# Recommender tower: block transposes and four of a chunk's 50 summations on VectorE, part of the last layer 1 earlier

## The reference, cut to what matters

```python
# 2048 samples, 40 fields; each field has a table of 1000 to 125000 rows of 32 floats
e = jnp.stack([tbl_0[ids[:, 0]], ..., tbl_39[ids[:, 39]]], axis=1)        # 2048 x 40 x 32
z = einsum('bke,kef,bkf->bk', e[:, I], W, e[:, J])                       # 780 pairs i < j, W is 780 x 32 x 32
h = concatenate([z, dense_ctx], axis=1)                                  # 796 columns
h = maximum(h @ W_top1 + b_top1, 0)                                      # 512
h = maximum(h @ W_top2 + b_top2, 0)                                      # 256
y = h @ W_top3                                                           # 1
```

## Time and profile before

| | us |
|---|---|
| median of 3 runs | 684.99 (684.2 to 687.2) |
| profiled execution, its own time | 685.17 |
| its span | 683.6 |
| TensorE busy (share of the span) | 660.2 (97%) |
| VectorE busy | 522.0 (76%) |
| ScalarE busy | 232.9 (34%) |
| GpSimd busy | 433.1 (63%) |

### The profile page before, as it was taken

How to read it: one execution, slowest core, us unless ns; L and a number is a source line. 1 busy time by engine, 2 the same in 40 slices (tenths; PEclk the granted TensorE clock), 3 DMA queues, 4 the chain that set the end, 5 groups by cost and what they waited for, 6 DMA issues and landing times.

```text
span 683.6 us, 13973 instructions
## 1 busy us (share of the span) xinstructions
PE 660.2 (97%) x5920; PEld 192.6 (28%) x5920; DVE 522.0 (76%) x483; ACT 232.9 (34%) x200; POOL 433.1 (63%) x452
## 2 busy tenths in 40 slices
PE   5679999999999999999999999999999999999998
PEld 1222323222322333222332233322222222222232
DVE  5687889999967668778987887568978778688900
ACT  6636675164554338630164313501010110010002
POOL 6777777777777777777777777777777774000000
PEclk9999999999999999999999999999999999999999
DMA  7832022111221021111222102001022210000000
GB/s 261 299 87 60 14 75 75 18 26 29 78 62 30 14 60 33 41 29 30 45 52 57 45 14 45 13 15 30 14 57 50 46 29 9 16 17 0 3 3 1
DMA packets 26454, 32.22 MB, mean 47 GB/s; under 512 B 10436, under 2 KB 18372, under 8 KB 26136
## 3 DMA queue, kind: packets, MB, share of 16 engines
q1 hardware_dynamic: 11736, 23.41, 11.1%
q0 software_dynamic: 14336, 7.37, 7.1%
q10 hardware_dynamic: 320, 0.56, 0.3%
HBM read 20.75 MB, written 0.06 MB: 30 GB/s over the span
## 4 chain that ended last, share of the span: by engine, by line
PE 94%; ACT 3%; DVE 1%; issue 1%; DMA 1%; ACTq 0%; DVEq 0%
PE t_ps L637 30%; PE z_ps L667 27%; PE x_ps L686 11%; PE x_ps L597 9%; PE t_ps L686 4%; PE t_ps L645 3%; PE x_ps L699 3%; PE x_ps L613 2%; PE t_ps L597 2%; ACT one_hot L460 1%; ACT one_hot L463 1%; PE x_ps L710 1%; PE t_ps L699 1%; DMA z_sb<-hot_tables 1%; DVE prod L555 0%
## 5 line engine op out<-in xcount | busy, mean ns | idle before, releaser
L555 DVE TENSOR_TENSOR prod<-t_ps,e_t 128x1024 f32<-128x1024 f32 x400 | 466.8, 1218 | 107.8 <-PE t_ps L637 76.1
L415 POOL DMA_INDIRECT rows<-tbl,idx x448 | 432.9, 966 | 139.9 <-issue 135.9
L637 PE MATMUL t_ps<-e_t,w_sb 32*128 32x512 f32 x1440 | 219.8, 640 | 1.1 <-DVE prod L555 1.0
L667 PE MATMUL z_ps<-prod,select 128*32 128x512 f32 x1600 | 207.8, 600 | 2.3 <-DVE prod L555 1.8
L637 PEld LDWEIGHTS t_ps<-e_t,w_sb 32*128 32x128 f32 x1440 | 65.9, 182 | 140.1 <-DVE prod L555 75.0
L460 ACT ACTIVATE one_hot<-hot_sb,row_number 128x2048 bf16<-128x2048 f16 (+1 forms) x44 | 85.4, 1940 | 36.6 <-PE x_ps L597 34.7
L686 PE MATMUL x_ps<-z_sb,w_sb 128*32 128x512 f32 x672 | 83.4, 597 | 0.7 <-ACT e_t L472 0.7
L463 ACT ACTIVATE one_hot<-one_hot 128x2048 bf16<-128x2048 bf16 (+1 forms) x44 | 81.5, 1853 | 1.4
L597 PE MATMUL x_ps<-one_hot,tables 128*32 128x512 bf16 x1074 | 72.7, 387 | 1.7 <-DVE tables L521 1.0
L667 PEld LDWEIGHTS z_ps<-prod,select 128*32 128x32 f32 x1600 | 39.3, 108 | 122.1 <-issue 61.6
L497 ACT COPY z_sb<-z_ps 128x512 f32<-128x512 f32 x28 | 16.4, 586 | 159.3 <-PE z_ps L667 159.2
(11 more groups left out here) (27 smaller groups left out, 83.8 us busy)
## 6 DMA issues: line engine op xcount, KB each, us to landing
rows<-tbl,idx POOLq DMA_INDIRECT x448, 2.3
hot_sb<-hot_ids SPq DMA_DIRECT2D x10, 512.0 KB
e_t<-e_t SPq DMA_DIRECT2D x80, 64.0 KB
e_t<-e_t SPq DMA_DIRECT2D x40, 128.0 KB
w_sb<-w_lay SPq DMA_DIRECT2D x1, 1792.0 KB
z_sb<-hot_tables SPq DMA_DIRECT2D x4, 320.0 KB, 6.2
w_sb<-w_lay SPq DMA_DIRECT2D x1, 1152.0 KB, 8.8
w_sb<-w_lay SPq DMA_DIRECT2D x1, 896.0 KB, 6.2
```

The lines of the kernel that those rows point to most:

```text
L415: pool.indirect_dma_start(out=rows[:, slot, t, E * f:E * f + E], out_offset=None, in_=tables[PER * c + f], in_offset=bass.IndirectOffsetOn ...
L555: nc.vector.tensor_tensor(prod[:, u % PROD_SLOTS, :, :], t_ps[:, at:at + 2, :], by, ALU.mult).then_inc(mult_done, 1)
L637: mm = nc.tensor.matmul(t_ps[:, at + r % 2, :], w_sb[part, b, :], e_t[part, e_slot(k, g), :], start=True, stop=True)
L667: mm = nc.tensor.matmul(z_ps[E * q:E * q + E, :], select[:, E - PER - PER * s:2 * E - PER - PER * s], prod[:, u % PROD_SLOTS, q % 2, :], s ...
```

## The change

- **Block transposes.** `turn` goes from TensorE to VectorE (L654): one instruction transposes 128 x 512 in blocks of 32 x 32 straight into `e_t`, and the copy by ScalarE goes. So that blocks are enough, a gather now fetches 32 samples of all four fields (4 x 32 rows, from one table in which the 28 large ones lie end to end), still 16 for an item, 448 in all. VectorE first adds each table's first row to the indices (L593), and GpSimd and the first cast (L596) come behind that addition.
- **Sums.** Bursts 9, 19, 25 and 31 of each chunk are not summed by `red`, but by VectorE (L663): a `tensor_reduce` that transposes blocks, one for each unit of 1024 elements, 32 in all. A block transpose (L671) brings a chunk's sums into z's layout, and an addition (L684) joins them with the four bursts of the same bank that `red` summed; it takes the place of ScalarE's copy of that bank.
- **Early layer 1.** In the last chunk banks 0 to 3 of layer 1 go through `x_ps` among the bursts, ScalarE keeps them in `h1_sb`, and VectorE adds them to the rest (L677).
- **Halves.** All `gen` steps are 8 products of 32 x 64, as those of L645 were.
- **Layer 3** is 4 products over 128 samples in four column groups (L829).
- **The string ORDER is new.** 70 of the 112 one-hot matrices are made by ScalarE (44 before), 42 by VectorE (68 before). In the list, between the first burst of chunk 0 and that of chunk 1 stand now 48 lookup blocks (43 before), 45 summations (48), 8 `turn` (7), 11 one-hot matrices on VectorE (25) and 8 sums; behind the first burst of chunk 1 stand 20 `turn` (21), 139 summations (152), 110 `layer1` (112) and 48 lookup blocks (50).

```diff
+HOT = [3, 3, 3, 3]
...
+CHUNKS = 4
+EARLY = 4
+SMALL = Z_BANKS - 2
+SMALL_SLOTS = BATCHES - (Z_BANKS - 1) * Z_SLOTS
+SUMMED = [9, 19, 25, 31]
+REDUCED = [b for b in range(len(BURSTS)) if b not in SUMMED]
+JOINED = SMALL - 1
+DENSE_AT = PER * SMALL_SLOTS
...
+def z_place(b):
+    if b in SUMMED:
+        return JOINED, Z_SLOTS - len(SUMMED) + SUMMED.index(b)
+    n = REDUCED.index(b)
+    if n >= SMALL * Z_SLOTS - len(SUMMED):
+        n += len(SUMMED)
+    if n >= SMALL * Z_SLOTS + SMALL_SLOTS:
+        n += Z_SLOTS - SMALL_SLOTS
+    return divmod(n, Z_SLOTS)
...
-    layer1 += [("layer1", chunks - 1, m, kb) for kb in range(Z_BANKS) for m in range(H1_TILES)]
+    layer1 += [("layer1", chunks - 1, m, kb) for m in range(H1_TILES) for kb in range(EARLY)]
+    layer1 += [("layer1", chunks - 1, m, kb) for kb in range(EARLY, Z_BANKS) for m in range(H1_TILES)]
...
+        "r": [("red", k, b) for k in range(chunks) for b in REDUCED],
+        "d": [("sum", k, b, half) for k in range(chunks) for b in SUMMED for half in range(2)],
+        "a": [("join", k) for k in range(chunks if SUMMED else 0)],
+        "t": [("turn", k, c) for k in range(chunks) for c in range(HOT[k], GROUPS)],
...
+        if k == CHUNKS - 1 and step[3] < EARLY:
+            return ("h1 early", k, step[2]), step[3] == 0, step[3] == EARLY - 1
+        return ("h1", k, step[2]), step[3] == (EARLY if k == CHUNKS - 1 else 0), step[3] == Z_BANKS - 1
...
+    GATHER = 16 * SPANS
...
+        idx = sb("idx", [P, len(items), SPANS], I32)
+        idx_raw = sb("idx_raw", [P, len(items), SPANS], I32)
+        if SUMMED:
+            sums = sb("sums", [P, SPANS, Z_SLOTS, PER])
...
+        def wait_for_products(engine, u):
+            if u >= PROD_SLOTS:
+                k, b = divmod((u - PROD_SLOTS) // 2, len(BURSTS))
+                if b in SUMMED:
+                    engine.wait_ge(sum_done, summed_to(k, b, u % 2))
+                else:
+                    engine.wait_ge(red_done, reduced_to(k, b))
...
-            pool.wait_ge(idx_loaded, 16)
-            for n, (k, c) in enumerate(items):
+            pool.wait_ge(idx_made, 1)
+            for n in range(len(items)):
                 slot = n % ROW_SLOTS
                 if n >= ROW_SLOTS:
-                    pool.wait_ge(x_made, use_no["e", *items[n - ROW_SLOTS]] + 1)
-                for t in range(TILES):
-                    for f in range(PER):
-                        pool.indirect_dma_start(
-                            out=rows[:, slot, t, E * f:E * f + E], out_offset=None,
-                            in_=tables[PER * c + f],
-                            in_offset=bass.IndirectOffsetOnAxis(
-                                ap=idx[:, k * TILES + t, PER * c + f:PER * c + f + 1], axis=0),
-                        ).then_inc(gathered[slot], 16)
+                    pool.wait_ge(turned, n - ROW_SLOTS + 1)
+                for span in range(SPANS):
+                    pool.indirect_dma_start(
+                        out=rows[:, slot, span, :], out_offset=None, in_=table,
+                        in_offset=bass.IndirectOffsetOnAxis(ap=idx[:, n, span:span + 1], axis=0),
+                    ).then_inc(gathered[slot], 16)
...
+                    if use[0] == "h1 early":
+                        nc.scalar.copy(h1_sb[:, m, :], bank_of(use)).then_inc(x_taken, 1)
+                    else:
+                        into = bank_of(use)
+                        if k == chunks - 1:
+                            act.wait_ge(h1_joined, m + 1)
+                            into = h1_sb[:, m, :]
+                        nc.scalar.activation(h1_sb[:, m, :], into, ACT.Relu,
+                                             bias=b1_sb[:, m:m + 1]).then_inc(x_taken, 1)
...
-                    nc.scalar.copy(y_sb[:, :], x_ps[0:1, :]).then_inc(x_taken, 1)
+                    nc.scalar.copy(y_sb[:, :], x_ps[:, 0:P]).then_inc(x_taken, 1)
...
+                nc.vector.memset(sums[:, :, :, :], 0.0).then_inc(sums_cleared, 1)
+            dve.wait_ge(idx_loaded, 16)
+            dve.wait_ge(numbers_loaded, 16)
+            nc.vector.tensor_tensor(idx[:, :, :], idx_raw[:, :, :], first_row.unsqueeze(2).broadcast_to(idx.shape),
+                                    ALU.add).then_inc(idx_made, 1)
...
+                elif kind == "turn":
+                    c = step[2]
+                    n = item_no[k, c]
+                    dve.wait_ge(gathered[n % ROW_SLOTS], (n // ROW_SLOTS + 1) * GATHER)
+                    wait_for_place(dve, k, c)
+                    nc.vector.transpose(e_t[:, e_slot(k, c), :],
+                                        rows[:, n % ROW_SLOTS, :, :].rearrange("p s e -> p (s e)")).then_inc(turned, 1)
+                elif kind == "sum":
+                    b, half = step[2:]
+                    u = first_unit(k, b) + half
+                    kb, s = z_place(b)
+                    dve.wait_ge(mult_done, u + 1)
+                    if b == SUMMED[0] and half == 0:
+                        dve.wait_ge(z_turned, k) if k else dve.wait_ge(sums_cleared, 1)
+                    nc.vector.tensor_reduce(sums[:, :, s, 2 * half:2 * half + 2].rearrange("p n q -> p q n"),
+                                            prod[:, u % PROD_SLOTS, :, :].rearrange("p q (n e) -> p q n e", e=E),
+                                            axis=mybir.AxisListType.X, op=ALU.add,
+                                            apply_transpose=True).then_inc(sum_done, 1)
+                    if b == SUMMED[-1] and half:
+                        bank = k * Z_BANKS + kb
+                        dve.wait_ge(sum_done, summed_to(k, b, half))
+                        wait_for_z_place(dve, bank)
+                        nc.vector.transpose(z_sb[:, bank % Z_RING, :],
+                                            sums[:, :, :, :].rearrange("p n s q -> p (n s q)")).then_inc(z_turned, 1)
+                elif kind == "layer1" and k == chunks - 1 and step[3] == Z_BANKS - 1:
+                    m = step[2]
+                    dve.wait_ge(x_taken, use_no["h1 early", k, m] + 1)
+                    dve.wait_ge(x_made, use_no["h1", k, m] + 1)
+                    nc.vector.tensor_tensor(h1_sb[:, m, :], t_ps[:, tail_banks["h1", k, m], :], h1_sb[:, m, :],
+                                            ALU.add).then_inc(h1_joined, 1)
+                elif kind == "join":
+                    bank = k * Z_BANKS + JOINED
+                    last = max(b for b in REDUCED if z_place(b)[0] == JOINED)
+                    dve.wait_ge(z_turned, k + 1)
+                    dve.wait_ge(red_done, reduced_to(k, last))
+                    nc.vector.tensor_tensor(z_sb[:, bank % Z_RING, :], z_ps[:, :], z_sb[:, bank % Z_RING, :],
+                                            ALU.add).then_inc(z_read, 1)
...
-            def turn(step):
-                _, k, c = step
-                use, _, _ = use_of(step)
-                open_bank(use)
-                slot, rounds = item_no[k, c] % ROW_SLOTS, item_no[k, c] // ROW_SLOTS
-                pe.wait_ge(gathered[slot], (rounds + 1) * GATHER)
-                for t in range(TILES):
-                    mm = nc.tensor.transpose(x_ps[:, t * P:(t + 1) * P], rows[:, slot, t, :], ident[:, :])
-                mm.then_inc(x_made, 1)
...
-                    pe.wait_ge(x_taken, use_no["e", k, g] + 1)
+                    wait_for_e(pe, k, g)
...
-                    if g < c:
-                        mm = nc.tensor.matmul(t_ps[:, at + r % 2, :], w_sb[part, b, :], e_t[part, e_slot(k, g), :],
+                    near = far = e_slot(k, g)
+                    if g == c:
+                        near, far = e_slot(k, c + r // 2), fold_slot(k, c + r // 2)
+                    for side in range(2):
+                        source = far if (r, side) in ((1, 0), (3, 1)) else near
+                        cols = slice(P // 2 * side, P // 2 * side + P // 2)
+                        mm = nc.tensor.matmul(t_ps[cols, at + r % 2, :], w_sb[part, b, cols], e_t[part, source, :],
                                               start=True, stop=True)
-                    else:
-                        near, far = e_slot(k, c + r // 2), fold_slot(k, c + r // 2)
-                        for side in range(2):
-                            source = far if (r, side) in ((1, 0), (3, 1)) else near
-                            cols = slice(P // 2 * side, P // 2 * side + P // 2)
-                            mm = nc.tensor.matmul(t_ps[cols, at + r % 2, :], w_sb[part, b, cols], e_t[part, source, :],
-                                                  start=True, stop=True)
...
-                mm = nc.tensor.matmul(x_ps[0:1, :], w3_sb[:, j:j + 1], h2_sb[:, j, :], start=first, stop=ends)
+                for q in range(PER):
+                    mm = nc.tensor.matmul(x_ps[E * q:E * q + 1, 0:P], w3_sb[:, j:j + 1], h2_sb[:, j, P * q:P * q + P],
+                                          start=first, stop=ends)
...
```

(22 more changed lines are left out.)

152 lines of the change are left out of this document (86 added, 66 removed).

## The result

| | us |
|---|---|
| predicted | 646.0 (637 to 660) |
| measured, median of 4 runs | 644.37 (643.69 to 646.65) |
| the kernel before on the same chip, median of 4 | 685.34 (684.2 to 687.2) |
| ratio, with its 95% interval | 0.9406 (0.9373 to 0.9438) |
| the profiled execution of the changed kernel, its span | 646.65, 644.9 |

A forecast was written before the change was run, and what follows sets the result against it. The prediction took TensorE's list of steps as the bound over the whole, VectorE as chunk 0's pace. It summed 35.8 + 0.9 (start) + 145 (chunk 0) + 460.8 (rest) + 2 (waits) = 644.5 and predicted 646 us, range 637 to 660.

The forecast's parts named there:

- TensorE's list: TensorE's steps over the whole kernel: they bound the time and lose 41.6 us, from 683.6 to 642.0.
- The turns: 28 transposes leaving TensorE at 0.58 us each: 16.2 us, and 1.4 us that they waited.
- The halves: 180 `gen` steps in halves, 1.05 us against 1.08: 3.6 us off TensorE, bounds 0 and 5.4.
- Layer 3: 8 TensorE steps with column groups side by side, 0.95 to 0.3 us each: 5.2 us, and 0.3 at the end.
- The summations: 16 summations (4 x 4) leaving TensorE at 0.93 us each: 14.9 us.
- Early layer 1 removes nothing: Last chunk: 16 steps, 14 us, move ahead of the last product, and TensorE's list keeps its length.
- VectorE's list: VectorE over the whole: loses 19.0 us of one-hot matrices, gains 65.4 us of new work, 568 us busy.
- Over the whole it does not bind: VectorE's floor, 568 + 14 + 21 = 603 us, lies 39 us under TensorE, so VectorE isn't the bound.
- Chunk 0 in 145 us: First to 201st product: VectorE sets the pace, 140 us of work and 3% idle, against 149.8 before.
- The start: Ahead of the first product: the cast comes behind the index addition, moving the start and every gather by 0.9 us.
- The rest: From chunk 1's first product to the end: 498.0 less 37.2 us is 460.8, and 2 for `gen` waits behind sums.
- The costlier coupling: Rival: sums of up to 2.3 us and other VectorE work hold up the products, 654 to 672 us; chance 0.15.

The follow-up runs named there:

- run 5: Changed kernel with 28 times four TensorE transposes, whose result nothing reads, added beside VectorE's block transposes: 660.39 us, 16.0 slower than the changed kernel.
- run 2: Changed kernel with the 180 `gen` steps between different groups in full width again, 4 products of 128 columns: 647.8 us, 3.4 slower.
- run 4: Changed kernel with layer 3 again as one product over 512 samples in one column group: 648.26 us, 3.9 slower.
- run 1: Changed kernel with no burst summed by VectorE, all 50 of each chunk summed by TensorE: 674.76 us, 30.4 slower.
- run 3: Changed kernel without early layer 1, its 16 steps back behind the last product: 651.23 us, 6.9 slower.
- run 6: Changed kernel with each of VectorE's 32 sums made twice, the second into a spare tile: 674.9 us, 30.5 slower.
- run 8: Changed kernel with the first cast ahead of the index addition and a second id spread step earlier: 642.83 us, 1.5 faster.
- run 7: Changed kernel with the 8 sums of chunk 0 cut to 32 of their 512 samples: 642.73 us, 1.6 faster.

## Why the prediction was right, and where it wasn't

- **TensorE's list.** Right: near 620 us forecast as busy, 618.5 measured. The turns were 16.2 us, and run 5 gives 16.0. The halves were 3.6, and run 2 gives 3.4. The Trainium skill, "TensorE: Matmul & The Clock Gate", Part 3, lets a weight load overlap matrix products in flight only where the row group differs, and the two halves share theirs. A `gen` in halves at 1.04 us, against 1.08 in full width, does not agree with it. Layer 3 was 5.5 with its smaller copy, and run 4 gives 3.9, though a step takes 0.22 and not my 0.3; part of a whole step runs beside its successor.
- **The summations.** 14.9 for 16 of them, 0.93 each. The undisturbed chunks of run 1 give 3.4 us for four, 0.85 each, which would be an estimated 13.6 for 16. The 30.4 of the whole run hold waits at the bank that the move itself made.
- **"Early layer 1 removes nothing; TensorE's own list keeps its length".** Wrong. It is worth 6.9 us (run 3). The two passages before it in my own text say why: a pair of `gen` and `red` costs TensorE 2.0 us and VectorE 2.3, and I counted 14 us in which VectorE had had nothing to do. In the stretch of pairs alone a `gen` takes at least 0.2 us more, and the early steps of layer 1 fill such holes: of their 14 us about 7 cost nothing. I left that out of the sum.
- **VectorE's list.** Right in its prices: a sum 1.23 against 1.18, a transpose 0.70 against 0.65, busy 566.2 against 568. The Trainium skill, "VectorE: DVE Perf Modes", The three transpose paths, gives 311 ns for one 128 x 128 transpose of bfloat16 in blocks, an estimated 1.24 us for an item of four; the measured 0.70 decides. The prediction read the advice of that page too widely: its Rules for kernel authors name TensorE for a full 128 x 128 transpose, and the transpose on VectorE as the fastest where blocks of 32 x 32 are enough, as they are here. They also call `tensor_reduce` VectorE's slowest operation; here a sum took 1228 ns, a product of that size 1214.
- **"Over the whole it does not bind, and the turns on it cost nothing but by place", with 39 us between the floors.** Wrong as a margin; for the change's own sums it held where it can be told. Run 6 uses 38.5 of the 39 us, and pays 28 to 30.5 for them, 0.73 to 0.79 for each. Two floors over the whole say nothing of a coupling by three banks: VectorE's free time is 76 waits of at most 3.0 us for TensorE (46.6 with smaller causes in the group of its products), 71 of them behind a lookup or a layer. A sum of 1.2 us that stands elsewhere isn't covered by them. The change's own sums still had room in chunks 2 and 3: by run 1 a summation moved away gave 0.85 of its 0.93 us there, so the coupling took at most 0.3 us a chunk, within the 2 us that I took. The same sums a second time cost 6.7 and 7.0 us in these two chunks.
- **Chunk 0 in 145 us, VectorE's pace.** 146.7 measured, with the dip of the clock; run 3 and run 8 show 144.2 and 144.9. The size was right, the mechanism in the main not: by run 7 VectorE's work can fall by 7 us without effect, and by run 5 TensorE's can't grow by 4.1 without costing 4.0. VectorE at 139 us stands close behind, which is why run 6 pays there. So the hit of this term is in part luck. That the gathers don't bind was right. (The product at 185.6 us, where the prediction ends the chunk before, is the 101st, not the 201st; the sum goes by 100 and is not touched.)
- **The start, 0.9 us.** It was 4.0. The addition took the 0.6 that I had given it (0.62), and the first gather came at 4.76, 0.6 later. What I missed is the chain through ScalarE. Its copy of the first ids came 1.5 us later (8.71), because a table's cast had meanwhile gone ahead of it, and so did the second id spread on TensorE; then 4.38 us of waiting for a one-hot matrix at 36.16, which ScalarE had begun only at 32.07, after 3.17 us of waiting for a load of ids. Behind that wait the granted clock was 0.54 from 37 to 42 us, where it had been 1.00 before the change. How much of the 4.0 each of these makes isn't shown. Run 8 takes 2.07 us of it back, and 1.5 in time.
- **The rest.** 462.8 forecast from chunk 1's first product to the end, 458.4 measured. The errors, +3.1 in the start, +1.7 in chunk 0 and -4.4 here, sum to 0.4 us in the span: part of the precision of the total is luck. Early layer 1, left out at 7.1, less 1.5 for layer 3 and 1.0 for 13 summations, makes 4.6 of it.
- **The rivals.** None came. The costlier coupling was the nearest: its mechanism is there, as run 6 shows, but not yet at 1.23 us for a sum.
